# A mixed-layer kernel: another order of the work between the recurrent layer and the mixture of experts

## The reference

```
x = layernorm(x + rwkv(x))            # k, v, r projections of x and its shifted copy, a scan over time,
                                      # out = (sigmoid(r) * wkv) @ Wo.T
x = layernorm(x + experts(x))         # router: top 2 of 8, softmax; silu(x Wg) * (x Wu), then Wd; width 176
x = layernorm(x + linear_attention(x))# elu + 1 features, 16 heads
x = layernorm(x + ternary_ffn(x))     # weights rounded to -1, 0, 1; sigmoid(x1) * x2; width 704
```

```
out = (e1 * num + e2 * vt) / (e1 * den + e2)
```

## Time and profile before

| | us |
|---|---|
| median of 3 runs | 431.73 |
| lowest, highest | 431.62, 432.14 |
| profiled execution, device time | 434.08 |
| its span, first to last instruction | 432.3 |
| PE busy | 384.6 (89%) |
| DVE busy | 294.3 (68%) |
| ACT busy | 205.9 (48%) |
| POOL busy | 129.5 (30%) |

### The profile page before, as it was taken

One profiled execution on the slowest core, in us unless ns is written; L12 is line 12 of the kernel. 1 busy time (PEld: TensorE's weight loads), 2 busy tenths in 40 slices (PEclk: granted clock), 3 DMA queues, 4 the chain that ended last, 5 costly groups with the idle time before them and its releaser, 6 DMA issues.

```text
span 432.3 us, 7368 instructions
## 1 busy us (share of the span) xinstructions
PE 384.6 (89%) x2260; PEld 332.9 (77%) x2260; DVE 294.3 (68%) x789; ACT 205.9 (48%) x419; POOL 129.5 (30%) x226
## 2 busy tenths in 40 slices
PE   3999999999739889999999868999999999999691
PEld 3888888888627677777777657988889889999690
DVE  4787999999982456687453255676868686866532
ACT  3374586558652433345335414554455544636341
POOL 2002256444632430003201167234435240401111
PEclk9999999999867999999999985999999999999977
DMA  6543954211122345733431131102020100000000
GB/s 210 184 172 127 137 207 146 70 37 50 49 76 94 99 153 150 247 98 100 134 111 50 52 94 52 50 0 74 4 72 27 49 27 2 24 2 25 2 26 24
DMA packets 28486, 35.70 MB, mean 83 GB/s; under 512 B 3680, under 2 KB 25632, under 8 KB 28192
## 3 DMA queue, kind: packets, MB, share of 16 engines
q1 hardware_dynamic: 19760, 21.72, 17.3%
q0 software_dynamic: 3072, 8.39, 6.0%
q10 hardware_dynamic: 5616, 5.11, 3.4%
HBM read 22.76 MB, written 12.45 MB: 81 GB/s over the span
## 4 chain that ended last, share of the span: by engine, by line
PE 49%; DVE 33%; issue 7%; ACT 6%; POOL 2%; another core or an unknown queue 1%; DMA 1%; SPq 0%; ACTq 0%; POOLq 0%; DVEq 0%
PE bank L394 20%; PE bank L535 10%; PE bank L556 8%; DVE st L1017 4%; PE bank L662 3%; PE bank L545 2%; PE bank L515 2%; PE bank L404 2%; DVE arena L1079 2%; PE bank L717 2%; DVE arena L1082 2%; DVE arena L1059 1%; DVE fl L1421 1%; DVE arena L1450 1%; DVE arena L1355 1%
## 5 line engine op out<-in xcount | busy, mean ns | idle before, releaser
L394 PE MATMUL bank<-arena 128*128 128x256 f32 (+2 forms) x576 | 120.2, 364 | 9.5 <-ACT arena L792 6.7
L394 PEld LDWEIGHTS bank<-arena 128*128 128x128 f32 x576 | 102.0, 195 | 23.4 <-issue 6.7
L778 ACT ACTIVATE arena<-bank 128x256 f32<-128x256 f32 (+1 forms) x118 | 45.5, 424 | 47.7 <-PE bank L556 26.4
L1538 POOL TENSOR_TENSOR ve<-mv,eps 128x2 f32<-128x2 f32 x32 | 7.0, 219 | 165.9 <-DVE mv L1021 165.9
L535 PE MATMUL bank<-gu,arena 128*128 x156 | 54.9, 476 | 0.0
L556 PE MATMUL bank<-dn,arena 96*128 x156 | 41.0, 385 | 4.6 <-DVE arena L1238 3.5
L783 ACT ACTIVATE arena<-arena,nm,rs 128x256 f32<-128x256 f32 x48 | 26.2, 597 | 38.7 <-POOL nm L1543 38.6
L1604 POOL DMA_INDIRECT arena<-yg,ypos x32 | 31.3, 978 | 39.0 <-DMA yg<-arena 30.6
L1238 DVE COPY arena<-bank 96x256 f32<-96x256 f32 x39 | 16.3, 419 | 39.1 <-PE bank L545 31.6
L556 PEld LDWEIGHTS bank<-dn,arena 96*128 96x128 f32 x156 | 28.7, 190 | 15.1 <-issue 7.0
L1578 POOL DMA_INDIRECT xg<-x,pos x32 | 34.3, 1073 | 14.7 <-issue 7.5
(11 more groups left out here) (207 smaller groups left out, 866.1 us busy)
## 6 DMA issues: line engine op xcount, KB each, us to landing
arena<-xg SPq DMA_DIRECT2D x39, 128.0 KB, 2.1
yg<-arena ACTq DMA_DIRECT2D x39, 128.0 KB
arena<-in_xT SPq DMA_DIRECT2D x8, 256.0 KB
x<-in_x SPq DMA_DIRECT2D x8, 256.0 KB, 4.4
out<-arena SPq DMA_DIRECT2D x8, 256.0 KB
gu<-in_w_gate SPq DMA_DIRECT2D x1, 1408.0 KB, 8.2
gu<-in_w_up SPq DMA_DIRECT2D x1, 1408.0 KB, 6.9
dn<-in_w_down SPq DMA_DIRECT2D x11, 128.0 KB, 6.0
```

Of the source, the lines that this page charges most:

```text
L394: last = pe.matmul(dst, l, r, start=i == 0, stop=i == len(pairs) - 1)
L778: return act.activation(dst, src, ACT.Copy)
```

## The change

No instruction is added or taken away. Five places get another order.

- PE: output(7) and logits(6) move ahead of gate_up(1) and turn(3). rank(6) goes between tile 0's front and back; turn_x1(7), logits(7), rank(7) and the second table's two products each come one tile earlier, or within another tile.
- ACT: turned(0) moves ahead of the reciprocal, turned(1) behind it, normalise_x1(6), turned(2) and copy_x1T(6) next, and only then the table load for silu. normalise_x1(7) moves ahead of tile 0.
- DVE: residual(7) and hidden(0) move ahead of choose(6), hidden(1) ahead of positions(6); the later gate products and copies change places with choose(7) and the table's steps.
- POOL: in the slot of index 8, weights(6) comes behind deviation(7) and no longer ahead of it.
- The loops over the remaining tiles on PE and DVE begin at 5, since tile 5 is no longer written out.

```diff
--- before.py
+++ after.py
@@ -588,28 +588,28 @@
             gate_up(0, experts[0])
             turn(2)
             turn_x1(B - 2)
+            output(B - 1)
+            logits(B - 2)
             gate_up(1, experts[1])
             turn(3)
-            logits(B - 2)
-            output(B - 1)
+            tile_front(0)
             rank(B - 2)
-            tile(0)
-            tile(1)
+            tile_back(0)
             turn_x1(B - 1)
+            tile_front(1)
+            logits(B - 1)
+            tile_back(1)
             tile_front(2)
-            logits(B - 1)
-            tile_back(2)
-            tile_front(3)
             rank(B - 1)
             pe.wait_ge(asked_ok, taken_at)
             pe.matmul(bank[5][:, 0:E], ones[:, :], taken_e[:, :], start=True, stop=True).then_inc(looked_ok, 1)
+            tile_back(2)
+            tile_front(3)
+            tile_order(1, bank[6][:, 0:1])
             tile_back(3)
             tile_front(4)
-            tile_order(1, bank[6][:, 0:1])
+            tile_rows(1, bank[6][:, 8 * E:8 * E + 2 * SECOND], where2[:, :, :])
             tile_back(4)
-            tile_front(5)
-            tile_rows(1, bank[6][:, 8 * E:8 * E + 2 * SECOND], where2[:, :, :])
-            tile_back(5)
 
             def turn_x2(b):
                 pe.wait_ge(x_ok[1], b + 1)
@@ -618,7 +618,7 @@
                 past(pe, anT_ok, b)
                 transposes(x2[b % 2], halves(BANK_TURN)).then_inc(x2Tp_ok, 1)
 
-            for i in range(6, TILES):
+            for i in range(5, TILES):
                 tile_front(i)
                 if i == 10:
                     pe.wait_ge(wsum_ok, 3)
@@ -899,23 +899,23 @@
             exponentials(B - 1)
             gaps(B - 3)
             act.preload_act_table_set("natural_log_exp_and_others")
+            turned(0)
             reciprocal(B - 1)
+            turned(1)
             normalise_x1(B - 2)
+            turned(2)
+            copy_x1T(B - 2)
             act.preload_act_table_set("silu_and_others")
-            turned(0)
-            turned(1)
-            copy_x1T(B - 2)
             silu(0)
-            turned(2)
             silu(1)
+            gaps(B - 2)
             turned(3)
-            gaps(B - 2)
+            normalise_x1(B - 1)
             tile(0)
-            normalise_x1(B - 1)
+            copy_x1T(B - 1)
             tile(1)
-            copy_x1T(B - 1)
+            gaps(B - 1)
             tile(2)
-            gaps(B - 1)
             tile(3)
 
             def x2_high(b):
@@ -1362,23 +1362,21 @@
                 dve.tensor_tensor(xT_lo[:, :, :], halves(4), xT_hi[:, :, :].bitcast(F32), ALU.subtract).then_inc(x2l_ok, 1)
 
             finish_y(B - 1)
+            residual(B - 1)
+            hidden(0)
             choose(B - 2)
-            hidden(0)
-            residual(B - 1)
+            hidden(1)
             positions(B - 2)
             hidden_turned(0)
-            hidden(1)
-            hidden_turned(1)
-            hidden(2)
             dve.scalar_tensor_tensor(taken[:, :], order[:, 0:1], float(FIRST), valid[:, 0:1], ALU.is_lt,
                                      ALU.mult).then_inc(table_step, 1)
             dve.wait_ge(table_step, 5)
             dve.tensor_scalar(taken_e[:, :], pick_e[:, :], taken[:, :], None, ALU.mult).then_inc(asked_ok, 1)
+            hidden_turned(1)
+            hidden(2)
+            choose(B - 1)
             hidden_turned(2)
             hidden(3)
-            choose(B - 1)
-            hidden_turned(3)
-            hidden(4)
             positions(B - 1)
             counts = bank[6][:, 4 * E:5 * E]
             dve.tensor_tensor(table[:, T_PAD:T_PAD + E], counts, region0[:, :], ALU.add).then_inc(pads_ok, 1)
@@ -1390,13 +1388,13 @@
             dve.tensor_reduce(ntile[:, :], over[:, :, :], AX_X, ALU.add)
             dve.wait_ge(looked_ok, done_at)
             dve.tensor_copy(done[:, :], bank[5][:, 0:E])
+            hidden_turned(3)
+            hidden(4)
+            tile_places(1, where2, bank[6][:, 0:1])
             hidden_turned(4)
             hidden(5)
-            tile_places(1, where2, bank[6][:, 0:1])
-            hidden_turned(5)
-            hidden(6)
             tile_table(1, bank[6][:, 8 * E:8 * E + 2 * SECOND])
-            for i in range(6, TILES):
+            for i in range(5, TILES):
                 hidden_turned(i)
                 if i + 1 < TILES:
                     hidden(i + 1)
@@ -1580,10 +1578,12 @@
                             in_=x1[:, n, :], in_offset=None).then_inc(scat_ok if b < FULL_AT else scat2_ok, 16)
 
             for s in range(B + 2):
-                if 0 <= s - 2:
+                if 0 <= s - 2 and s != B:
                     weights(s - 2)
                 if 0 <= s - 1 < B:
                     deviation(0, s)
+                if s == B:
+                    weights(s - 2)
                 if 0 <= s - 2:
                     scatter(s - 2)
```

## The result

The changed kernel took 428.89 us (median of 6 runs, 427.39 to 429.81), the kernel before, on the same chip, 431.57 us (6 runs, 431.04 to 432.14): a ratio of 0.9935, 95% interval 0.9915 to 0.9954. It is faster, by 2.7 us and not by the 6.5 forecast; 428.89 lies above the range of 421.8 to 428.3. The profiled execution took 429.13 us with a span of 427.4.

The account below looks back on a forecast made before the run. TensorE, busy 89% of the span, was taken as the bound, so only its waits or half-clock time could be won. Gains 4.8 + 1.7 = 6.5 us; 431.7 − 6.5 = 425.2 us, range 421.8 to 428.3.

Parts of the forecast that it names:

- The copies and the restart: Tile 0's copy on ACT, moved ahead of the reciprocal, starts about 125.2; PE restarts at 125.72, 4.17 us earlier.
- The clock in the first block: PE's clock falls as before and returns at 130.4, after 4.7 us of unbroken products; output(7) ends at 131.95.
- DVE's chain: First block: residual(7) at 132.0, choose(6) at 133.9, then down(0) at 137.85 instead of 142.67; gain 4.8 us.
- The second table load: ACT's load of 1.28 us, about 130.4 to 131.7, has 1.6 us of cover before hidden(0) and costs nothing.
- The Trainium skill's drain: About 1.38 us beside ACT's table load by the page; silu(0)'s result then at 133.4 instead of 132.0, still covered.
- Behind down(0), gain 1.7: After the first down product, two PE waits go, 1.4 us, plus 0.3 for slower starts; 0 if they remain.
- waits of 0.29 and 1.10 us: Two later PE waits, last caused by DVE copies recorded late; the new order lets both go, 1.4 us.
- rival C: Clock returns late or new waits eat part; a late copy precedes choose(7), holding rank(7): gain 3.1 to 5 us; 22%.
- The prediction's own sign of being wrong: At batches 6 and 7: the forecast is wrong if choose(6) or choose(7) waits for logits while PE stands.
- The base: Whole kernel: the gain of 6.5 us was taken from the median, 431.7; the profiled execution took 434.08.
- The upper bound of the sum, 8.2: Largest total gain, in us, if PE's clock came back at once in the first block; output(7) ends at 130.7.

Follow-up runs that it names:

- chip C: One follow-up lot: changed kernel unedited, 421.98 us, ratio 0.9919 to the kernel before (425.78 us in its one further execution); also two edited versions, 0.999 and 0.9934.
- chips B and C: Two follow-up lots without late words; on B, three edits of the changed kernel (0.9896, 0.9907, 0.9986) and ACT's order alone in the kernel before (0.9889).
- chip A: The lot of the first pair: changed kernel 428.89 us against the kernel before, 431.57 us, ratio 0.9935.
- chip D: Follow-up lot: changed kernel 0.9972, with hidden_turned(0) ahead of positions(6) 0.995; kernel before with ACT's order 0.9926, with that copy moved too 0.9917.
- six lots: All runs, A to F, each one chip at one time, times compared within a lot only; the kernel before took 425.8 to 431.6 us.

## Why the prediction missed

**The copies and the restart: right.** Copy at 125.64 (about 125.2 was forecast), second transposes at 126.17 (125.72), the logarithm slipped by 0.43 and not by 0.1 at most, output products from 130.25 (129.80).

**The clock in the first block: the number right, by luck in part.** Low until 130.0:130.5, where 130.4 was forecast. But the forecast kept the clock high until 125.7, and it had been low since 116.6. In the kernel before, that earlier low stretch ended at 122.3, and PE's rank products show it:

```profile
122.47 0.39 PE L462 MATMUL bank<-seen,ones 128*128 128x16 f32 x2 [0.60 <-DVE seen L1129]
```

Nor do 4.7 us of unbroken products decide the return: from the second transposes of tile 0 to the return it was 4.1 us here, 3.5 in the changed kernel on C, and 5.5 with the copy behind the reciprocal. What the low clock costs in this block is 0.8 us on chip C, and 0.5 to 1.0 more where it lasts until 130 or 131.

**DVE's chain: right.** residual(7) 132.21 (132.0), choose(6) 134.11 (133.9), down(0) 138.10 (137.85): 4.57 us where 4.8 were forecast, against 4.85 on chip C. Both experiments that moved hidden_turned(0) confirm that this chain sets the point. The second table load was covered. The Trainium skill's drain ("ScalarE: Activation LUTs", What ACT_TABLE_LOAD costs) isn't there: silu(0) on ACT starts at 132.39, 1.30 us after the start of the load, which took 1.28.

**Behind down(0), gain 1.7: the step that failed.** I took the waits of 0.29 and 1.10 us in the kernel before for waits that the order makes, and let both go. They are not: the copies that end them, at 149.08 and 159.18, were themselves waiting for words of PE, whose transposes had ended 1.9 us before at 147.16 and 157.29; both words came only when the scatters of batches 6 and 7 had been issued. With the words on time (chips B and C) both orders take 16.3 us there, and the term is zero. On chip A the changed order draws the scatter of batch 6 forward as well, from 143.34 to 137.92, and its end now falls on logits(7): the lateness passes through choose(7) and rank(7), PE waits 0.99 us and the clock falls for 3.4 us. So the stretch grew by 1.06. In the place of +1.7 stands −1.06, 2.8 us of the 3.8 missing. The row that would have warned me was in my hands: DVE's copy at 149.08 starts 1.9 us after PE's record (147.16) had ended, with "remote" as releaser, and the prediction says only that such causes "are recorded late". The rival C (22%) came nearest: it had choose(7) holding up rank(7). But it blamed a late copy ahead of choose(7), and DVE stood idle for 2.85 us there, waiting for the logits; and its gain of 3.1 to 5 us is above the 2.7. The prediction's own sign of being wrong, "if choose(6) or choose(7) waits for logits while PE stands", came nearly so: choose(7) waited for its logits, and PE stood for 0.99 us just behind.

**The base.** I subtracted from the median a sum made against one execution, whose second low stretch was 13.7 us. The same kernel had 6.8 and 3.4 us of it on chip C. In the pair of profiled executions 1.44 came back behind tile 6, 1.1 of it by just behind that stretch (that the stretch is the cause is argued, not shown), and between the medians 2.27 went: 6.5 − 0.23 − 2.76 + 1.44 − 2.27 = 2.7. The upper bound of the sum, 8.2, was also too high by its own rows: output(7) at 130.7 instead of 131.95 adds 1.25, which makes 7.75.

**The order around PE, DVE and POOL** brings nothing that the runs can show: alone it has a ratio of 0.999, and ACT's part alone 0.9889 and 0.9926, where the whole change has 0.9919 to 0.9972 in five lots. On chip D ACT's order alone is 2.9 us faster than the whole change at the median, though the intervals of the two overlap. Of the versions tried I'd keep the kernel before with ACT's order and the copy ahead of positions(6); it had 0.9917 where ACT's order alone had 0.9926, which is no measurable difference.

Open: what holds the words up, whether it is bound up with the recording, why in some lots only, and what sets whether the clock falls near 400 us, which splits the runs of one kernel on one chip in two groups some 4 us apart.

## What to carry to other kernels

When a wait ends with a copy that is itself late, follow it one step further, to the end of the products that it reads. If those ended long before (here 1.9 us) and the copy's engine stood idle all the same, don't count the wait as one that another order removes, and look at the other engines' timelines at that moment. Look at what else the change draws forward, GpSimd's indirect DMAs among it, and where their end falls. And take a forecast's base from several executions, since one profile's low stretches of the clock can differ from another's by as much as the change is worth.

## What the runs showed of the hardware

- Near the end of GpSimd's indirect DMAs (four in 4.9 us, 137.92 to 142.79) some words of PE reached DVE and ACT only 0.7 to 1.0 us after the last one's end, in four of the six lots; words from earlier in the same four were on time. With eight in a row (9.9 us) one came 6.9 us after the products' end. On two chips with the same program none was late. The Trainium skill ("DMA: Bandwidth & Descriptors", Terms) says that with software descriptor generation the descriptors are written to rings in SBUF; no run here shows whether that is the cause.
- The same kernel, before, took 425.8 to 431.6 us (medians) in the six lots, 1.4% apart; of the 8.4 us between its two profiled executions (PE's last product at 423.34 and 414.95) the late words make 1.95 us behind down(0) (18.25 and 16.30). At four later groups of indirect DMAs (the one at 212.16 to 216.93, and those that end at 297.41, 318.07 and 338.72) PE's words are late again on A and on time on C, and the distance of the same ACT instructions in the two traces grows by 0.55 to 0.67 us around each: by this estimate some 2.4 us more.
- In the same four lots, and not in the other two, the trace lost 57 to 73 of 1364 records of semaphore updates, all around GpSimd's indirect DMAs. A lost record is not a late word: in the changed kernel most words of 151.06 to 153.29 lack their record, and their readers started on time.
- 16 fp32 products of 8 columns (32 records) took 3.64 us at the high clock, which fell only at 117.6, behind them; 32 of them took 10.57, of which 7.2 at the low clock (low from 117.0).
